# Scores computed twice, with the causal mask added inside VectorE's minimum, in a fused attention and mixture-of-experts kernel

## The chip, the cores and the metric

The program runs on one core of one Trainium2 chip. The metric is the device time of one execution in microseconds (us). Engines are named as in the profile: PE is TensorE's matmul queue and PEld its weight loads, DVE is VectorE, ACT is ScalarE, POOL is GpSimd, SP is the queue of SyncE, which here only issues DMAs.

## The reference

```python
B, S, D = 8, 512, 256          # 8 sequences of 512 tokens, 16 heads of 16
x = x + attention(x @ cond_weight[itok[b]].T + cond_bias[itok[b]])   # causal softmax(Q K^T / 4) V, then W_o
h = relu(x @ wi.T + two low-rank terms) @ wo.T + two low-rank terms   # 1024 hidden units
gates = softmax(h @ gate_w + gate_b); top 2 of 8 experts per token
out = x + sum over the two of gate * (gelu(gelu(h @ w1 + b1) @ w2 + b2) @ w3 + b3)
```

All of it is float32. For one head the attention is

```python
scores = Q @ K.T / DH ** 0.5 + triu(-inf, k=1)
out = softmax(scores, axis=-1) @ V
```

## The kernel before

The program has two parts. The first takes the 8 sequences one after the other. Round b does the attention of sequence b together with the feed-forward part of sequence b-1, so there are 9 rounds: round 0 has attention only, round 8 feed-forward only. The second part, which the change does not touch, sorts the tokens by expert and runs 71 tiles of 128 tokens through the experts.

A round has an **opening** and then a number of **steps**. In the opening PE makes q, k and v of the sequence (each product as three matmuls of a high and a low part), the products with `wo_sb` and `sel_sb`, and the first hidden units of the sequence before. Then come 35 steps. A step takes two units; a unit is one head of one tile of 128 queries, and there are 64. For each unit PE adds the mask to PSUM with a bf16 matmul (`mask_b`, `id_b`) and then the scores (`q_sb`, `k_sb`, 64 rows of the array, so that two heads stand above each other). DVE takes the negated maximum of the row (`nmax`), ACT computes the exponential and its sum (`probs`), PE transposes `probs` block by block (line 831), DVE or ACT copies the result to `probs_t`, and every other step PE multiplies four heads with `v_sb` into bank 6. Into each step goes one **filler**, a piece of the feed-forward work (`FILLERS`).

Every engine runs its own list in order; PSUM banks are handed over by two semaphores each (`filled` and `drained`, with `vacant` before a bank is used again). The score ring has banks 0, 1 and 2. The last product of a round before the next one opens is in bank 1 (`rt`).

Besides this the rounds split the experts' weights for the second part, 8 **pieces** of 128x512 a round, 64 in all. A piece goes through this circle, with one buffer `w_rest` and one buffer `w_high`: POOL issues the load of `w_rest` from HBM (line 1513); ACT rounds it to `w_high` (line 990, `cast`); POOL subtracts, in place (line 1516); POOL issues two stores to `wsplit` (line 1521); when both have landed, POOL issues the next load. ACT's `cast` stands at fixed places in ACT's list, two in the opening (`W_OPENING`) and six in the steps:

```python
W_OPENING = (0, 10)
W_STEPS = (2, 8, 14, 19, 23, 28)
...
            def cast(b, n):
                act.wait_ge(s_wpiece, b * (16 * W_PIECES) + 16 * (n + 1))
                nc.scalar.copy(w_high[:, :], w_rest[:, :]).then_inc(s_whigh, 1)
...
                if piece or not isinstance(b, int) or b:
                    pool.wait_ge(s_wsplit, n * 32)
```

## Time and profile before

| | |
|---|---|
| Median of 3 runs | 1509.88 us (1509.63 to 1516.31) |
| The profiled execution | 1507.66 us, of which the trace spans 1506.1 us |
| PE busy | 1359.4 us, 90% of the span |
| DVE, ACT, POOL busy | 875.0, 767.0, 420.0 us |
| Mean granted clock of PE | 0.955 of full speed |
| First part (rounds 0 to 8) | up to about 937 us |
| Exponentials on ACT, maxima on DVE | 266.0 us and 227.3 us |
| Transposes of `probs` on PE (x1280) | 203.1 us |

The span is what the trace covers; the profiled execution's own time is 1.6 us above it. Busy time of a group of instructions counts each moment once within the group, while neighbours overlap, so what an instruction costs in a full queue is the distance of the starts and not its duration.

### The profile page before, as it was taken

The numbers are of one execution on the slowest core, as the hardware profiler recorded it, in microseconds if no ns is written. First come the engines' busy times: TensorE is split into PE (matmuls) and PEld (weight loads), VectorE is DVE, ScalarE is ACT, GpSimd is POOL, SyncE is SP. The second block draws the span as 40 slices with busy tenths as digits, with TensorE's granted clock in tenths as the row PEclk, the third lists the DMA queues.
The fourth block names the chain that finished last, engine by engine and source line by source line (L and its number), as shares of the span: only waits on it lengthen the run. The fifth ranks groups of instructions, "written<-read, shape, count | busy, mean of one in ns | idle before, by whom it ended". The sixth has DMA issues, their size and how long they took to land.

```text
span 1506.1 us, 32247 instructions
## 1 busy us (share of the span) xinstructions
PE 1359.4 (90%) x10297; PEld 1053.1 (70%) x10298; DVE 875.0 (58%) x1945; ACT 767.0 (51%) x2003; POOL 420.0 (28%) x553
## 2 busy tenths in 40 slices
PE   5989999999989989999999988249899999999997
PEld 3556766766766766766766757238788888888886
DVE  3765665665665665665666662645455555555554
ACT  4776676665666665675666651013233333333332
POOL 2212211221221211211212210133344444444442
PEclk9799999999999999999999999559999999999999
DMA  6112222222222222222222220652624223342221
GB/s 221 64 66 97 76 82 98 78 96 82 78 95 83 77 81 93 77 86 98 78 80 77 79 72 29 271 225 36 247 42 145 42 42 88 101 148 40 38 40 13
DMA packets 50642, 137.85 MB, mean 92 GB/s; under 512 B 10514, under 2 KB 29586, under 8 KB 48882
## 3 DMA queue, kind: packets, MB, share of 16 engines
q0 software_dynamic: 28992, 68.35, 16.9%
q1 hardware_dynamic: 21554, 68.18, 12.3%
q8 instruction: 65, 1.06, 0.3%
q14 instruction: 31, 0.25, 0.1%
HBM read 86.03 MB, written 51.38 MB: 91 GB/s over the span
## 4 chain that ended last, share of the span: by engine, by line
PE 81%; DVE 5%; ACT 4%; issue 4%; DMA 4%; POOL 1%; SPq 0%; POOLq 0%; DVEq 0%; ACTq 0%
PE bank L665 66%; PE bank L831 9%; PE bank L924 4%; ACT probs L1092 3%; DVE nmax L1276 2%; PE bank L916 1%; DMA xg<-hrows,gid 1%; DMA w_rest<-in_w_all 1%; DMA wsplit<-w_rest 1%; POOL hit_v L1536 0%; PE bank L839 0%; ACT w_high L990 0%; DVE probs_t L1290 0%; POOL w_rest L1516 0%; PE bank L779 0%
## 5 line engine op out<-in xcount | busy, mean ns | idle before, releaser
L1092 ACT ACTIVATE probs<-bank,nmax 128x512 f32<-128x512 f32 (+3 forms) x512 | 266.0, 525 | 164.4 <-DVE nmax L1276 163.0
L1276 DVE TENSOR_REDUCE nmax<-bank 128x1 f32<-128x512 f32 (+3 forms) x512 | 227.3, 486 | 201.7 <-PE bank L665 201.3
L1128 ACT ACTIVATE g<-z 128x512 f32<-128x512 f32 x142 | 89.8, 632 | 281.3 <-DVE z L1466 270.0
L831 PE MATMUL bank<-id_f,probs 128*128 128x128 f32 x1280 | 203.1, 290 | 0.4 <-ACT probs_t L1100 0.4
L1516 POOL TENSOR_TENSOR w_rest<-w_rest,w_high 128x512 f32<-128x512 f32 x64 | 81.4, 1271 | 425.5 <-ACT w_high L990 425.5
L665 PE MATMUL bank<-wst,g1t_high 128*128 x568 | 186.0, 409 | 0.9 <-DVE g1t_low L1454 0.9
L831 PEld LDWEIGHTS bank<-id_f,probs 128*128 128x128 f32 x1280 | 137.8, 143 | 45.0 <-issue 24.2
L1558 POOL DMA_INDIRECT out<-y_sb,sid x71 | 114.3, 1610 | 149.7 <-PE bank L916 67.1
L1290 DVE COPY probs_t<-bank 128x128 f32<-128x128 f32 (+3 forms) x320 | 140.1, 454 | 12.6 <-PE bank L831 12.6
L1466 DVE TENSOR_TENSOR z<-bank,b_sb 128x512 f32<-128x512 f32 x142 | 98.2, 692 | 74.3 <-PE bank L665 63.2
L665 PEld LDWEIGHTS bank<-wst,g1t_high 128*128 128x128 f32 x568 | 102.5, 190 | 20.8 <-issue 1.1
L665 PE MATMUL bank<-wst,g1t_low 128*128 x284 | 113.4, 399 | 0.0
L665 PE MATMUL bank<-wst,g2t_high 128*128 x568 | 107.7, 289 | 1.5 <-DVE g2t_low L1454 1.5
L665 PE MATMUL bank<-k_sb,q_sb 64*128 64x512 f32 (+3 forms) x512 | 107.8, 418 | 0.0
L665 PE MATMUL bank<-mask_b,id_b 128*128 128x128 bf16 x512 | 84.6, 228 | 21.2 <-ACT probs L1092 17.4
L1092 ACT ACTIVATION_READ_ACCUMULATOR probs<-bank,nmax 128x1 f32 x512 | 101.3, 198 | 0.0
L665 PE MATMUL bank<-probs_t,v_sb 128*32 128x128 f32 x2560 | 98.4, 281 | 0.0
L665 PE MATMUL bank<-wst,xgt_high 128*128 x284 | 96.9, 423 | 1.3 <-DVE xgt_low L1454 1.3
L1513 POOL DMA_DIRECT2D w_rest<-in_w_all x64 | 35.0, 546 | 216.4 <-DMA wsplit<-w_rest 216.4
L1548 POOL DMA_INDIRECT xg<-hrows,gid x71 | 76.2, 1073 | 63.8 <-POOL gid L1545 56.8
L665 PEld LDWEIGHTS bank<-probs_t,v_sb 128*32 128x32 f32 x2560 | 62.9, 110 | 41.9 <-issue 28.4
L1100 ACT COPY probs_t<-bank 128x384 f32<-128x384 f32 (+3 forms) x192 | 88.3, 460 | 3.1 <-PE bank L831 2.9
(213 smaller groups left out, 2879.2 us busy)
## 6 DMA issues: line engine op xcount, KB each, us to landing
wst<-wsplit SPq DMA_DIRECT2D x8, 4096.0 KB, 12.6
w_rest<-in_w_all POOLq DMA_DIRECT2D x64, 256.0 KB, 3.1
wsplit<-w_high POOLq DMA_DIRECT2D x64, 256.0 KB, 2.3
wsplit<-w_rest POOLq DMA_DIRECT2D x64, 256.0 KB, 2.6
hrows<-h_sb SPq DMA_DIRECT2D x8, 528.0 KB, 3.0
x_in<-in_xT SPq DMA_DIRECT2D x8, 512.0 KB, 3.5
wb_raw<-in_lora_wb SPq DMA_DIRECT2D x8, 512.0 KB, 3.5
x_res<-in_xT SPq DMA_DIRECT2D x8, 512.0 KB, 4.5
```

The costliest lines, as they stand in the source:

```text
L665: return nc.tensor.matmul(*a, **k)
L831: ins = nc.tensor.transpose(at(n, rd)[:, kb * P:(kb + 1) * P], probs[:, t % 4, kb * P:(kb + 1) * P], id_f[:, :])
L924: ins = nc.tensor.transpose(bank[bt][:, k * P:(k + 1) * P], g[:, k * P:(k + 1) * P], id_f[:, :])
L1092: taken(nc.scalar.activation(probs[:, s % 4, 0:(i + 1) * P], at(n, rd)[:, 0:(i + 1) * P], ACT.Exp, bias=nmax[:, s % 8:s % 8 + 1], accum_ou ...
L1100: taken(nc.scalar.copy(probs_t[:, t % PT_SLOTS, 0:w], at(n, rd)[:, 0:w]), n, rd)
L1128: nc.scalar.activation(g[:, :], z[:, :], ACT.Gelu).then_inc(s_g, 1)
L1276: V.tensor_reduce(nmax[:, s % 8:s % 8 + 1], at(n, rd)[:, 0:(s // HEADS + 1) * P], AX.X, ALU.max, negate=True).then_inc(s_max, 1)
L1290: taken(V.tensor_copy(probs_t[:, t % PT_SLOTS, 0:w], at(n, rd)[:, 0:w]), n, rd)
L1466: V.tensor_tensor(z[:, :], bank[bl][:, :], bias[:, bass.ds(e, 1), :].rearrange("p o n -> p (o n)"), ALU.add).then_inc(s_z, 1)
L1516: nc.gpsimd.tensor_tensor(w_rest[:, :], w_rest[:, :], w_high[:, :].bitcast(F32), ALU.subtract).then_inc(s_wlow, 1)
L1548: nc.gpsimd.indirect_dma_start(xg[:, buffer, :], None, hrows, bass.IndirectOffsetOnAxis(ap=gid[:, 0:1], axis=0), bounds_check=B * S - 1, o ...
L1558: nc.gpsimd.indirect_dma_start(out_rows, bass.IndirectOffsetOnAxis(ap=sid[:, 0:1], axis=0), y_sb[:, buffer, :], None, bounds_check=B * S - ...
```

## The change

Two heads (a pair) are taken at a time over all 512 queries, in three chunks each, and the scores are computed twice. The first time they have the queries on the partitions: DVE adds a causal mask to the negated scores and keeps the minimum of each row, in one instruction per tile (`tensor_tensor_reduce`, which is followed by an instruction that reads the accumulator), so PE's mask matmul is gone. The minima go, as a high and a low part, through a matmul with an identity into two more rows of `q_sb` (rows 32, 33 and 96, 97), against ones in `k_sb`. The second time PE computes the scores with the keys on the partitions (`st`), with the maximum already in the sum: ACT takes the exponential straight into `probs_t`. So PE's transposes, the copies to `probs_t` and ACT's reads of its accumulator are gone. POOL zeroes what lies above the diagonal (`affine_select`, line 1578 of the new kernel, four of 128x256 for each pair). The row sums come out of the product with `v_sb`, which holds ones now; a matmul with `swap_sb` brings them beside the values (`nn`), and DVE takes the reciprocal of 128x512 and multiplies. A round has 34 steps; `FILL_COUNTS` says how many fillers each has. POOL's part is written out for all rounds, without a loop. The buffer `x_res` is gone, so `load_res` stands later in SP's list.

The casts: none in the opening, and one at steps 9, 12, 15, ..., 30.

```diff
-W_OPENING = (0, 10)
-W_STEPS = (2, 8, 14, 19, 23, 28)
...
+SCORE_CHUNKS = ((3,), (2, 0), (1,))
+KEY_CHUNKS = ((0,), (3, 1), (2,))
...
+M_LAG, ST_LAG, PV_LAG, NORM_LAG = 4, 5, 12, 20
+STEPS = NORM_LAG + 2 + 6 * (QUADS - 2)
...
+def work_at(step):
+
+
+    return (chunk_at(step), chunk_at(step - ST_LAG), every(step - M_LAG, CHUNKS, PAIRS),
+            every(step - PV_LAG, 2 * CHUNKS, QUADS), every(step - NORM_LAG, 4 * CHUNKS, KD))
...
+FILL_COUNTS = [2] * 5 + [1] * 7 + [0] + [1] * 5 + [0, 1, 0, 1, 1, 1, 0] + [2] * 5 + [0, 1, 0, 1]
...
+CAST_LAG = 9
```

PE, in each step:

```diff
+                    score, late, m, quad, norm = work_at(step)
+                    if score is not None:
+                        g, u = score
+                        if u == 0:
+                            drained(pe, ("qs", g), rd)
+                            drained(pe, ("ks", g), rd)
+                        for half in range(2):
+                            n = ("s", g, u, half)
+                            vacant(pe, n, rd)
+                        for c, (i, cols) in enumerate(query_tiles(u)):
+                            for half in range(2):
+                                n, r = ("s", g, u, half), STRIP * half
+                                ins = mm(at(n, rd)[:, cols], q_sb[r:r + STRIP, g, i * P:(i + 1) * P],
+                                         k_sb[r:r + STRIP, g, 0:(i + 1) * P], start=True, stop=True,
+                                         skip_group_check=True)
+                                if c == len(SCORE_CHUNKS[u]) - 1:
+                                    done(ins, n, rd)
+                    if late is not None:
+                        g, u = late
+                        if u == 0:
+                            drained(pe, ("m", g), rd)
+                        for half in range(2):
+                            vacant(pe, ("st", g, u, half), rd)
+                        for c, (kb, cols) in enumerate(key_tiles(u)):
+                            for half in range(2):
+                                n, r = ("st", g, u, half), STRIP * half
+                                ins = mm(at(n, rd)[:, cols], k_sb[r:r + STRIP, g, kb * P:(kb + 1) * P],
+                                         q_sb[r:r + STRIP, g, kb * P:S], start=True, stop=True, skip_group_check=True)
+                                if c == len(KEY_CHUNKS[u]) - 1:
+                                    done(ins, n, rd)
+                    if m is not None:
+                        n = ("m", m)
+                        vacant(pe, n, rd)
+                        pe.wait_ge(s_msplit, b * PAIRS + m + 1)
+                        for i in range(TB):
+                            ins = mm(at(n, rd)[:, i * P:(i + 1) * P], mm_sb[:, 2 * i:2 * i + P], id_r[:, :],
+                                     start=True, stop=True)
                         done(ins, n, rd)
...
+                    if norm is not None:
+                        n = ("nn", norm)
+                        vacant(pe, n, rd, [("pv", 2 * norm + 1)])
+                        done(mm(at(n, rd)[:, :], swap_sb[:, :], sums[:, :], start=True, stop=True), n, rd)
+                    for n_fill, piece in rd.fillers(step):
+                        product(rd, n_fill, piece)
+                    if quad is not None:
+                        n = ("pv", quad)
+                        vacant(pe, n, rd, [("v", t2) for t2 in range(TB // 2)] if quad == 0 else ())
+                        pe.wait_ge(s_pmask, 2 * (b * PAIRS + 2 * (quad + 1)))
+                        for kb in range(TB):
+                            for c in range(4):
+                                h = 4 * quad + c
+                                values = v_sb[:, kb, quad // 2, c, quad % 2:quad % 2 + 2, :]
+                                first = PT_AT[kb]
+                                ins = mm(at(n, rd)[PART * c:PART * (c + 1), kb * P:S],
+                                         values.rearrange("p a d -> p (a d)"),
+                                         probs_t[:, h % PT_SLOTS, first:first + S - kb * P],
+                                         start=(kb == 0), stop=(kb == TB - 1))
                         done(ins, n, rd)
```

ACT, in each step:

```diff
+                    _, late, m, quad, _ = work_at(step)
+                    if late is not None:
+                        g, u = late
+                        if u == 0 and g >= 3:
+                            filled(act, ("pv", (g - 3) // 2), rd)
+                        for half in range(2):
+                            n = ("st", g, u, half)
+                            width = key_tiles_width[u]
+                            filled(act, n, rd)
+                            taken(nc.scalar.activation(probs_t[:, (2 * g + half) % PT_SLOTS, S * u:S * u + width],
+                                                       at(n, rd)[:, 0:width], ACT.Exp, scale=-1.0), n, rd)
+                    if m is not None and m % 2 == 0:
+                        n = ("m", m)
+                        filled(act, n, rd)
+                        for half in range(2):
+                            rows = slice(STRIP * half + M_ROW, STRIP * half + M_ROW + 2)
+                            ins = nc.scalar.copy(q_sb[rows, m, :], at(n, rd)[rows, :])
+                        taken(ins, n, rd)
+                    for n_fill, piece in rd.fillers(step):
+                        take(rd, n_fill, piece)
+                    if quad is not None and quad % 2 == 0:
+                        n = ("pv", quad)
+                        if quad:
+                            filled(act, ("nn", quad // 2 - 1), rd)
+                        filled(act, n, rd)
+                        nc.scalar.activation(ot_sb[:, quad // 2, :], at(n, rd)[:, :], ACT.Identity, scale=marks_sb[:, 1:2])
+                        taken(nc.scalar.activation(sums[:, :], at(n, rd)[:, :], ACT.Identity, scale=marks_sb[:, 2:3]),
                               n, rd)
...
+                    cast_of = every(step - CAST_LAG, CHUNKS, PAIRS)
+                    if cast_of is not None:
+                        cast(b, cast_of)
                     if step in LORA_STEPS:
                         lora_high(b, *LORA_STEPS[step])
```

DVE, in each step:

```diff
+                    score, _, m, _, norm = work_at(step)
+                    quad = work_at(step - 1)[3]
+                    if quad is not None and quad % 2 == 1:
+                        n = ("pv", quad)
+                        drained(dve, ("pv", quad - 1), rd)
                         filled(dve, n, rd)
...
+                        V.scalar_tensor_tensor(ot_sb[:, quad // 2, :], at(n, rd)[:, :], marks_sb[:, 2:3],
+                                               ot_sb[:, quad // 2, :], ALU.mult, ALU.add)
+                        taken(V.scalar_tensor_tensor(sums[:, :], at(n, rd)[:, :], marks_sb[:, 1:2], sums[:, :],
+                                                     ALU.mult, ALU.add), n, rd)
+                    if score is not None:
+                        g, u = score
+                        for half in range(2):
+                            n = ("s", g, u, half)
+                            filled(dve, n, rd)
+                            dve.sem_inc(s_tick, 1)
+                            for i, cols in query_tiles(u):
+                                ins = V.tensor_tensor_reduce(at(n, rd)[:, cols], at(n, rd)[:, cols],
+                                                             mask_w[:, S - (i + 1) * P:S], 1.0, 2.0 * BIG,
+                                                             ALU.add, ALU.min, nmax[:, g % 2, half, i:i + 1])
+                            taken(ins, n, rd)
+                        if u == CHUNKS - 1:
+                            drained(dve, ("s", g, u, 1), rd)
+                            if g > 0:
+                                filled(dve, ("m", g - 1), rd)
+                            V.tensor_scalar(m_parts(0), nmax[:, g % 2, :, :], -1.0, None, ALU.mult).then_inc(s_mhigh, 1)
+                            dve.wait_ge(s_mhigh, b * PAIRS + g + 1)
+                            V.scalar_tensor_tensor(m_parts(1), nmax[:, g % 2, :, :], -1.0, m_parts(0).bitcast(F32), ALU.mult,
+                                                   ALU.subtract).then_inc(s_msplit, 1)
+                    if m is not None and m % 2 == 1:
+                        n = ("m", m)
+                        filled(dve, n, rd)
+                        for half in range(2):
+                            rows = slice(STRIP * half + M_ROW, STRIP * half + M_ROW + 2)
+                            ins = V.tensor_copy(q_sb[rows, m, :], at(n, rd)[rows, :])
+                        taken(ins, n, rd)
                     if norm is not None:
...
+                        n = ("nn", norm)
                         filled(dve, n, rd)
...
+                        taken(V.reciprocal(rt_sb[:, :], at(n, rd)[:, :]), n, rd)
+                        drained(dve, n, rd)
+                        V.tensor_tensor(ot_sb[:, norm, :], ot_sb[:, norm, :], rt_sb[:, :], ALU.mult).then_inc(s_ot, 1)
+                    for n_fill, piece in rd.fillers(step - 1) if step > 0 else ():
                         take(rd, n_fill, piece)
                     if step in LOW_STEPS:
```

POOL:

```diff
+            def allowed(rd, g, u, tiles):
...
+                drained(pool, ("st", g, u, 1), rd)
+                at_0, at_1 = (PT_AT[kb] // P for kb in tiles)
+                for half in range(2):
+                    blocks = probs_t[:, (2 * g + half) % PT_SLOTS, :].rearrange("p (n c) -> p n c", c=P)
+                    diag = blocks[:, at_0:at_1 + 1:at_1 - at_0, :]
+                    ins = nc.gpsimd.affine_select(diag, diag, [[0, 2], [1, P]], ALU.is_ge, 0.0, base=0,
+                                                  channel_multiplier=-1)
+                ins.then_inc(s_pmask, 1)
...
+            def load_piece(b, piece):
+                cols = slice(piece * W_PIECE, (piece + 1) * W_PIECE)
+                if b or piece:
+                    pool.wait_ge(s_wsplit, (b * W_PIECES + piece) * 32)
+                pool.dma_start(w_rest[:, :], w_all[b:b + 1, :, cols].rearrange("o p n -> (o p) n")).then_inc(s_wpiece, 16)
...
+            def split_piece(b, piece):
                 n = b * W_PIECES + piece
                 cols = slice(piece * W_PIECE, (piece + 1) * W_PIECE)
...
                 pool.wait_ge(s_whigh, n + 1)
                 nc.gpsimd.tensor_tensor(w_rest[:, :], w_rest[:, :], w_high[:, :].bitcast(F32), ALU.subtract
                                         ).then_inc(s_wlow, 1)
                 pool.wait_ge(s_wlow, n + 1)
...
                 for part, src in enumerate((w_high[:, :].bitcast(F32), w_rest[:, :])):
...
+                    pool.dma_start(wsplit[b:b + 1, :, part, cols].rearrange("o p n -> (o p) n"), src
                                    ).then_inc(s_wsplit, 16)
 
...
+            for b in range(B):
+                rd = Round(b)
+                for g in range(PAIRS):
+                    allowed(rd, g, 1, (0, 3))
+                    load_piece(b, g)
+                    allowed(rd, g, 2, (1, 2))
```

What the change makes of ACT's list between two casts. Rows of before, a round with feed-forward work, two casts that follow each other in the steps:

```order
L990 CAST w_high<-w_rest 128x512
L1092 ACTIVATE probs,rsum<-bank,nmax 128x256 x2
L1092 ACTIVATE probs,rsum<-bank,nmax 128x384 x2
L1100 COPY probs_t<-bank 128x256
L1092 ACTIVATE probs,rsum<-bank,nmax 128x384 x2
L1100 COPY probs_t<-bank 128x384
L1115 COPY rt_sb<-bank 128x256
L1092 ACTIVATE probs,rsum<-bank,nmax 128x384 x2
L1100 COPY probs_t<-bank 128x384
L1092 ACTIVATE probs,rsum<-bank,nmax 128x384 x2
L1100 COPY probs_t<-bank 128x384
L990 CAST w_high<-w_rest 128x512
```

Rows of the change, the same engine and a round of the same kind, from one cast to the one after the next (`q_sb` here is the copy of the minima, 2x512):

```order
L1019 CAST w_high<-w_rest 128x512
L1128 ACTIVATE probs_t<-bank 128x256 x2
L1128 ACTIVATE probs_t<-bank 128x512 x4
L1019 CAST w_high<-w_rest 128x512
L1128 ACTIVATE probs_t<-bank 128x256 x2
L1135 CAST q_sb<-bank 2x512 x2
L1128 ACTIVATE probs_t<-bank 128x512 x4
L1019 CAST w_high<-w_rest 128x512
```

Between these two casts ACT had the work of five steps; now it has six exponentials, the work of three steps.

POOL's list for one piece, before:

```order
L1513 DMA w_rest<-in_w_all 128x512
L1516 TENSOR_TENSOR w_rest<-w_rest,w_high 128x512
L1521 DMA wsplit<-w_high 128x512
L1521 DMA wsplit<-w_rest 128x512
L1513 DMA w_rest<-in_w_all 128x512
```

and after:

```order
L1586 DMA w_rest<-in_w_all 128x512
L1578 AFFINE_SELECT probs_t<-probs_t 128x2x128 x2
L1592 TENSOR_TENSOR w_rest<-w_rest,w_high 128x512
L1596 DMA wsplit<-w_high 128x512
L1596 DMA wsplit<-w_rest 128x512
L1578 AFFINE_SELECT probs_t<-probs_t 128x2x128 x2
L1586 DMA w_rest<-in_w_all 128x512
```

The circle of a piece stands as it was; two selects have come in on each side of the load.

PE's list at the end of a round, after the change (`gw_sb` is the gate, `sums` the `nn` product in bank 0, `wq_high` the next round's first product, also in bank 0):

```order
L684 MATMUL bank<-probs_t,v_sb 32x512 x4
L684 MATMUL bank<-probs_t,v_sb 32x384 x4
L684 MATMUL bank<-probs_t,v_sb 32x256 x4
L684 MATMUL bank<-probs_t,v_sb 32x128 x4
L684 MATMUL bank<-gw_sb,ht_sb 128x8 x8
L684 MATMUL bank<-sums,swap_sb 128x512
L684 MATMUL bank<-cond_high,wq_high 128x512
```

Between the `nn` product and the next opening PE has nothing any more, and the opening's first product takes the bank of `nn`.

## Rows read from the trace of the kernel before

**Rows 1.** Timeline of PE, first instructions of rounds and of round 0's steps (start, duration).

```profile
32.63 0.27 PE L665 MATMUL bank<-mask_b,id_b 128*128 128x128 bf16 x2 [1.74 <-DVE k_sb L1198]
...
111.77 0.47 PE L665 MATMUL bank<-cond_high,wq_high 128*128 128x512 f32 x1 [1.48 <-DVE cond_low L1188]
...
785.51 0.47 PE L665 MATMUL bank<-cond_high,wq_high 128*128 128x512 f32 x1 [1.56 <-issue]
...
890.55 5.33 PE L665 MATMUL bank<-ot_sb,wo_sb 128*128 128x512 f32 x8 [1.46 <-DVE ot_sb L1282]
```

**Rows 2.** Windows, round 3's opening and steps: us, PE, PEld, DVE, ACT, POOL, PEclk.

```profile
331.90:359.00 27.10, 24.41 (x122) 17.21 (x122) 14.44 (x25) 12.55 (x25) 5.81 (x8) 0.94 0.37 127
359.00:442.00 83.00, 79.63 (x769) 58.94 (x768) 53.61 (x132) 56.50 (x174) 17.50 (x24) 1.00 0.22 75
```

**Rows 3.** Chain that ended last, round 3, one piece (start, duration).

```profile
403.76 1.29 POOL w_rest L1516
406.35 4.38 DMA wsplit<-w_rest
410.94 0.53 issue
411.49 3.09 DMA w_rest<-in_w_all
```

**Rows 4.** Timeline of POOL, round 0, the shortest circle of a piece.

```profile
28.58 1.28 POOL L1516 TENSOR_TENSOR w_rest<-w_rest,w_high 128x512 f32<-128x512 f32 x1 [3.54 <-ACT w_high L990]
...
31.01 0.54 POOL L1521 DMA_DIRECT2D wsplit<-w_rest  x1
34.19 0.54 POOL L1513 DMA_DIRECT2D w_rest<-in_w_all  x1 [2.64 <-DMA wsplit<-w_rest]
38.22 1.27 POOL L1516 TENSOR_TENSOR w_rest<-w_rest,w_high 128x512 f32<-128x512 f32 x1 [3.49 <-ACT w_high L990]
```

**Rows 5.** Waits, whole span (us in total, times, longest).

```profile
POOL w_rest L1513 <- DMA wsplit<-w_rest: 216.4, 63, 6.1
...
ACT w_high L990 <- DMA w_rest<-in_w_all: 13.5, 9, 2.2
```

**Rows 6.** Timeline of ACT, the second cast of round 3's opening.

```profile
345.78 0.62 ACT L990 CAST w_high<-w_rest 128x512 fp32r<-128x512 f32 x1 [1.38 <-DMA w_rest<-in_w_all]
```

**Rows 7.** Windows, PE's gap in that opening and behind it.

```profile
344.00:348.00 4.00, 1.39 (x11) 0.62 (x10) 1.69 (x4) 2.48 (x5) 1.26 (x1) 0.97 0.17 55
348.00:352.00 4.00, 4.00 (x16) 3.32 (x16) 1.24 (x3) 0.60 (x1) 1.10 (x2) 0.61 0.36 131
```

**Rows 8.** Timeline of PE, a step with 512-wide tiles and the gate.

```profile
322.16 0.51 PE L665 MATMUL bank<-k_sb,q_sb 64*128 64x512 f32 x2
322.60 1.09 PE L831 MATMUL bank<-id_f,probs 128*128 128x128 f32 x8
323.53 1.02 PE L665 MATMUL bank<-x_in,wc_sb 128*128 128x512 f32 x2
324.48 1.08 PE L665 MATMUL bank<-probs_t,v_sb 128*32 128x128 f32 x32
...
326.42 1.85 PE L665 MATMUL bank<-gw_sb,ht_sb 128*128 128x8 f32 x16
```

**Rows 9.** Timeline of PE, two matmuls of 512 columns back to back.

```profile
353.46 0.39 PE L665 MATMUL bank<-x_low,wi_high 128*128 128x512 f32 x1
353.69 0.39 PE L665 MATMUL bank<-x_high,wi_low 128*128 128x512 f32 x1
```

**Rows 10.** Groups by line and form, round 3, ACT and DVE (busy, mean ns).

```profile
L1092 ACT ACTIVATE probs<-bank,nmax 128x512 f32<-128x512 f32 x16 | 10.9, 685 | 5.5 <-DVE nmax L1276 5.5
...
L1276 DVE TENSOR_REDUCE nmax<-bank 128x1 f32<-128x512 f32 x16 | 10.3, 686 | 7.0 <-PE bank L665 7.0
...
L1301 DVE RECIPROCAL rinv<-rsum 128x16 f32<-128x16 f32 x4 | 1.0, 246 | 0.0
...
L1241 DVE RECIPROCAL ginv<-gsum 128x4 f32<-128x4 f32 x1 | 0.2, 178 | 0.0
```

356 lines of the change are left out of this document (137 added, 219 removed).

## The prediction

> **What bounds the kernel now.** I read the rounds first. PE's first instruction of round 1 is at 111.77 us, that of round 7 at 785.51, and round 8 begins its product with `wo_sb` at 890.55 [rows 1]: rounds 1 to 6 take (785.51 - 111.77) / 6 = 112.3 us each, round 0's steps 79.1 us (from 32.63), round 7 up to that product 105.0 us. The windows over round 3 show PE busy for 24.4 of 27.1 us in the opening and 79.6 of 83.0 us in the steps, at a granted clock of 0.94 and 1.00, with DVE and ACT at about 54 and 57 of those 83 us [rows 2]. So PE sets the pace. But the chain through the same round leaves PE once, for a piece of the expert weights: POOL's subtraction at 403.76, the landing of its stores, the next load, 3.09 us until that has landed [rows 3]. This second limit lies close below the first, and the change moves both.
>
> **The circle of a piece.** From the subtraction of one piece to that of the next nothing can overlap, since `w_rest` is one buffer. The shortest in the trace runs from 28.58 to 38.22, 9.64 us [rows 4]: 2.97 us from the subtraction to the end of the second store's issue apart from the wait, 2.64 us until the stores have landed, 4.03 us from the load's issue to the next subtraction, with ACT's cast in it. The wait for the stores is 216.4 / 63 = 3.43 us on the mean [rows 5]; in round 3 the part from the load on is 3.8 us (3.09 us of landing [rows 3], the cast of 0.62 us [rows 6] and a handover of 0.1). I take 2.97 + 3.43 + 3.9 = **10.3 us**. Eight of them fit into 112.3 us, so ACT waited for a load only 9 times in 64, 13.5 us in all [rows 5].
>
> **What three steps cost now.** After the change eight casts stand at steps 9, 12, ..., 30: seven circles must pass within 21 steps. What would the 21 steps take without them? PE loses, per round, 160 transposes at 0.93 / 8 = 0.116 us, 18.6 us; 32 mask pairs at about 0.2 us (0.27 us busy [rows 1]), 6.7 us; and the `rt` transposes, 1 us. It gains the second scores, 24 pairs of chunks at no more than 0.44 us, 10.6 us; 32 identity products, priced as transposes of the same size, 3.7 us; and two `nn` products at 0.95 us, 1.9 us [rows 8]. The columns through `v_sb` are as many as before. That is 10 us less, 94 us of PE in a round of which 22 us are opening: 34 steps at 2.1 us, three steps about **6.4 us**. The circle needs 10.3. ACT waits at each cast, and behind the cast in its list stand the exponentials of the next steps; their PSUM banks (4 and 5, one chunk's worth) stay full, and PE can go about one step further. So the circle sets the pace of steps 9 to 30.
>
> DVE stays under this. Per pair of heads it has eight fused instructions over 2560 columns, at the reduction's 686 ns for 512 [rows 10] about 3.9 us with the accumulator reads, and some 1.5 us of small work. That this instruction is as fast as the reduction is not shown anywhere; were it to take twice as long, a pair would cost some 9 us, still below 10.3. POOL's four selects per pair are one-input operations on 256 columns; the nearest row is its subtraction of 512 with two inputs, 1.27 us [rows 4], so between half of that and all, 0.64 to 1.27 us. Two stand in the wait for the stores (3.43 us) and two in the wait for load and cast (3.3 us); up to 1.3 us each, both waits cover them. I take 0.64.
>
> **A round after the change, from PE's first product.**
> - Opening: 27.1 us now. The cast in it kept ACT for 1.38 + 0.62 = 2.0 us [rows 6], in front of `low_i`; PE stood still for 2.6 of the 4 us from 344 and ran the next 4 us at a clock of 0.61 [rows 7], which loses 4 x 0.39 = 1.6 us. With the cast gone, 2.0 and 1.6 us go: 23.5 us.
> - Steps 0 to 8: nine score chunks and four second ones at 0.44, two identity groups 0.9 us, 44 matmuls of 512 columns at 0.23 us [rows 9] and 16 transposes: 18.7 us, and a tenth at each change of work, 20 us; a wait of about 1 us for the copy of the minima, which DVE makes behind its minima. Step 9 up to the cast: scores 0.9 us and two exponentials of at most 0.69 us [rows 10], 2.2 us. Together 23.2 us.
> - Seven circles: 72.1 us.
> - End: the product with `v_sb` of the last four heads waits for POOL's selects of the last pair, which stand behind the last load: 0.7 + 2.97 + 3.43 + 0.54 + 1.3 = 8.9 us after the cast before the last, 1.4 us ahead of the last cast. It has 40 blocks of 128 columns where the row has 16 in 1.0 us [rows 8], 2.6 us; gate 1.8 us; `nn` 0.95 us. Then PE has nothing to do: the next round's first product takes the bank of `nn`, which DVE frees only when the reciprocal is done. Its price is not in the trace for this size: 16 elements take 246 ns and 4 take 178 ns [rows 10], 5.7 ns an element, so 178 + 508 x 5.7 = 3.1 us; were it an ordinary operation, 0.69 us. The two rows point to the long one and I take it. End: 7.2 us after the last cast.
> - The gap before the opening is as long as the one in rows 7, so 1.6 us more at the lower clock.
>
> Sum: 23.5 + 1.6 + 23.2 + 72.1 + 7.2 = 127.6 us, 15.3 us more than 112.3. Six rounds: +92 us. Round 0: about 22.5 us to the first cast (DVE's fused instructions and the base weights' low parts set it), 72.1 and 5.4 us without a gate, 100.0 against 79.1: +21 us. Round 7: 128.4 up to the product with `wo_sb` against 105.0: +23 us. A microsecond for the longer preparation of round 0. In all +137 us on the span of 1506.1 us, that is 1643; outside of it lie 1.6 us (1507.66), and the median of the runs shown is 2.2 us above that execution: **1647 us**.
>
 The two small rows give 5.4 cycles an element; no row has the large size.
>
> **Rivals.**
> 1. PE goes on setting the pace and the kernel is faster. For it speaks that PE is the bound in rows 2 and loses 10 us a round. Then a round takes some 13 us less (10, the 3.6 us of the opening, less 1 for the reciprocal), and the kernel 1507.7 - 8 x 13 = 1404 us. It needs a circle that ends within three steps; what decides is 112.3 = 55.5 + 7 x circle, 8.1 us. Against it: the shortest of 63 is 9.64 us, and nothing in it has been removed. 0.04. A circle of about 8.1 us, no change: 0.03.
> 2. The steps are even slower than the circle. PE works 6.4 us in each 10.3 us and stands still twice in two circles, since every second one it also waits for the selects before the product with `v_sb` (8.9 us after a cast). Behind that wait stand this product, two steps and the next chunk, 8.9 us at full clock: 17.8 of 20.6 us. At half clock they are 16.8 us and two circles 25.7 us, 18 us more a round, 1790 us at worst. Rows 7 show the clock back after 4 us of dense work, so I give it 0.12, for 1715 to 1790 us. The Trainium skill (TensorE: Matmul & The Clock Gate, section on HAM oscillation) describes just such a kernel, in which a DMA wait between short bursts leaves every burst at the lower clock; the trace so far shows single gaps alone.
> 3. All is as I say, but every circle takes the shortest time and the rest of the round shrinks more: 1520 to 1590 us, 0.05.
>
> **How the numbers follow.** The forecast has 0.76, with a range of its own of 1590 to 1715 us. Below: all 56 circles at 9.64 us, -37 us, and the reciprocal at 0.69 us, -19 us. Above: every wait for the stores as in rows 3, from 406.35 + 0.54 to 411.49, 4.6 us and so 1.2 us more than the mean, +67 us. To hold 8 in 10 it takes in a little of rival 2: 1590 to 1725. A measurement of this kernel tells about 0.5%, 8 us. Faster 0.04, same 0.03, slower 0.93.
>
> **What the profile after will show.** If I am right: ACT's cast waits for the load of `w_rest` some 56 times, 3 to 5 us each, and this pair leads the list of waits; casts 10.3 us apart within a round; the chain made of landings of `wsplit` and `w_rest` for the greater part of the first 1050 us; PE busy well under 0.8 there, with a clock between 0.7 and 0.95; DVE's reciprocal near 3 us with PE idle behind it. Wrong would be: casts 6 to 7 us apart (the DMAs land sooner when they are issued from written-out code), or casts more than 12 us apart with ACT waiting for PE or for POOL instead. The second part must take the same 570 us as now.

## The result and the profile after

| | before | after |
|---|---|---|
| median of the runs | 1512.78 us | 1694.95 us |
| range of the runs | 1509.63 to 1516.31 (4) | 1686.55 to 1696.32 (4) |
| ratio | | 1.1206, interval 1.115 to 1.1261 |
| span of the profiled execution | 1506.1 us | 1684.8 us |
| rounds 1 to 6, each | 112.3 us [rows 1] | 133.7 us |
| round 7 up to the product with `wo_sb` | 105.0 us [rows 1] | 131.1 us |

The kernel is 12% slower; the forecast was 1647 us (1590 to 1725) and slower.

The page of the changed kernel, lines of its parts 1, 2 and 4 (busy time; PE's granted clock in 40 slices; the chain by engine and by line):

```profile
PE 1350.7 (80%) x7705; PEld 991.3 (59%) x7706; DVE 919.2 (55%) x2297; ACT 646.5 (38%) x1236; POOL 517.4 (31%) x809
...
PEclk8578877977978987978978897775899999999998
...
PE 60%; DMA 12%; DVE 11%; POOL 6%; issue 6%; ACT 4%; SPq 0%; POOLq 0%; DVEq 0%; ACTq 0%
```

The digits of the clock have a pattern that repeats with the rounds: two or three slices of 8 or 9 and then 7. The windows over rounds 1 to 6 say it in one number. The first fence is the kernel before, the second the changed one (us, then PE, PEld, DVE, ACT, POOL, PEclk, share of the DMA engines, GB/s):

```profile
111.77:785.51 673.74, 631.69 (x5521) 460.51 (x5521) 420.37 (x958) 430.87 (x1224) 139.93 (x192) 0.99 0.25 85
```

```profile
137.93:940.14 802.21, 628.72 (x3576) 415.42 (x3577) 452.17 (x1218) 338.95 (x645) 214.15 (x384) 0.84 0.20 70
```

PE has 35% fewer matmul records and the same busy time, because each takes longer. The share of the clock that was not granted is (1 - 0.84) x 802 = 128 us of these six rounds, against 7 us before. That is more than what it costs, since PE also stands still for 173 us of them (42 before), and a low clock costs nothing while it does. The same work on PE at a clock of 0.99 takes 547 us (run 11 below, 3579 records), so the lower clock makes PE's own work 629 - 547 = 82 us longer, 14 us a round.

The waits of the changed kernel (us in total, times, longest), which answer to [rows 5]:

```profile
ACT w_high L1019 <- DMA w_rest<-in_w_all: 115.3, 31, 8.0
...
POOL w_rest L1586 <- DMA wsplit<-w_rest: 96.5, 56, 5.1
PE bank L684 <- POOL probs_t L1578: 96.3, 23, 12.4
...
PE bank L684 <- DVE nmax L1335: 56.8, 51, 4.3
...
PE bank L684 <- DVE rt_sb L1357: 24.8, 7, 3.5
...
PE bank L684 <- DVE q_sb L1352: 22.7, 24, 1.0
```

ACT waited 9 times for a load before, now 31 times. PE's own waits are new kinds: for POOL's selects (in front of the product with `v_sb`), for DVE's minima, for the reciprocal and for DVE's copy of the minima into `q_sb`.

The eight casts of round 3 in ACT's timeline of the changed kernel (the second cast of a round in [rows 6] is the one that answers):

```profile
458.34 0.62 ACT L1019 CAST w_high<-w_rest 128x512 fp32r<-128x512 f32 x1
...
470.38 0.62 ACT L1019 CAST w_high<-w_rest 128x512 fp32r<-128x512 f32 x1
...
479.00 0.62 ACT L1019 CAST w_high<-w_rest 128x512 fp32r<-128x512 f32 x1 [1.12 <-DMA w_rest<-in_w_all]
...
487.66 0.62 ACT L1019 CAST w_high<-w_rest 128x512 fp32r<-128x512 f32 x1 [2.78 <-DMA w_rest<-in_w_all]
...
499.54 0.62 ACT L1019 CAST w_high<-w_rest 128x512 fp32r<-128x512 f32 x1
...
514.00 0.62 ACT L1019 CAST w_high<-w_rest 128x512 fp32r<-128x512 f32 x1
...
524.30 0.62 ACT L1019 CAST w_high<-w_rest 128x512 fp32r<-128x512 f32 x1 [3.56 <-DMA w_rest<-in_w_all]
...
532.95 0.62 ACT L1019 CAST w_high<-w_rest 128x512 fp32r<-128x512 f32 x1 [6.12 <-DMA w_rest<-in_w_all]
```

Four gaps end in a wait for the load, the second, third, sixth and last, and three, of 11.9 to 14.5 us, do not. Three of the four are 8.6 and 8.7 us long; the sixth is 10.3 us. Over the eight rounds the seven gaps add up to 73.9 us on the mean; by place they are 11.4, 8.6, 8.8, 10.6, 14.3, 11.0 and 9.0 us. The second gap in the chain that ended last, and the load of the sixth:

```profile
471.08 1.29 POOL w_rest L1592
472.37 0.29 issue
472.65 0.56 POOL wsplit L1596
473.21 2.58 DMA wsplit<-w_rest
475.79 0.29 issue
476.08 2.90 DMA w_rest<-in_w_all
478.97 0.02 issue
479.00 0.63 ACT w_high L1019
...
519.82 4.46 DMA w_rest<-in_w_all
```

It is the circle of [rows 3], shorter than there by 2.58 us of landing where 4.38 us stood, and 0.29 us to the next load where it was 0.53. The landing in [rows 3] is a late one: the pages of both kernels have the same median for this store (KB each, median us from issue to landing).

```profile
wsplit<-w_rest POOLq DMA_DIRECT2D x64, 256.0 KB, 2.6
```

The sixth gap is a circle too, one in which the load took 4.46 us to land instead of 2.90. And the end of the round in PE's timeline:

```profile
531.48 3.96 PE L684 MATMUL bank<-probs_t,v_sb 128*32 128x512 f32 x32 [7.48 <-POOL probs_t L1578]
535.38 1.95 PE L684 MATMUL bank<-gw_sb,ht_sb 128*128 128x8 f32 x16
537.18 1.10 PE L684 MATMUL bank<-sums,swap_sb 128*128 128x512 f32 x2
541.83 0.77 PE L684 MATMUL bank<-cond_high,wq_high 128*128 128x512 f32 x1 [3.54 <-DVE rt_sb L1357]
542.39 0.63 PE L684 MATMUL bank<-cond_low,wq_high 128*128 128x512 f32 x1
542.82 0.63 PE L684 MATMUL bank<-cond_high,wq_low 128*128 128x512 f32 x1
```

PE waits 7.48 us for the last selects, then 3.54 us for the reciprocal, and the products behind it follow each other at 0.43 us instead of the 0.23 us of [rows 9]: half clock.

### The profile page after: what moved, and what is told of

Its sections match the earlier page's. It is cut to its first block, busy times and chain, and to the rows that moved or that the text cites. A ratio compares the mean times of both kernels' runs of the same rounds, so it can differ in the third digit from the quotient of the medians.

```text
span 1684.8 us, 26627 instructions
## 1 busy us (share of the span) xinstructions
PE 1350.7 (80%) x7705; PEld 991.3 (59%) x7706; DVE 919.2 (55%) x2297; ACT 646.5 (38%) x1236; POOL 517.4 (31%) x809
## 4 chain that ended last, share of the span: by engine, by line
PE 60%; DMA 12%; DVE 11%; POOL 6%; issue 6%; ACT 4%; SPq 0%; POOLq 0%; DVEq 0%; ACTq 0%
PE bank L684 55%; DMA wsplit<-w_rest 6%; PE bank L953 4%; DMA w_rest<-in_w_all 3%; DVE rt_sb L1357 3%; POOL w_rest L1592 3%; DVE bank L1335 3%; ACT w_high L1019 1%; POOL wsplit L1596 1%; DVE q_sb L1352 1%; POOL probs_t L1578 1%; PE bank L945 1%; DMA xg<-hrows,gid 1%; ACT probs_t L1128 1%; POOL w_rest L1586 1%
## 5 line engine op out<-in xcount | busy, mean ns | idle before, releaser
L1335 DVE CUSTOM_DVE_ANT_0 bank<-bank,mask_w 128x512 f32<-128x512 f32 (+3 forms) x512 | 240.6, 517 | 134.5 <-PE bank L684 133.2
L1128 ACT ACTIVATE probs_t<-bank 128x512 f32<-128x512 f32 (+1 forms) x384 | 181.1, 524 | 223.0 <-PE bank L684 222.0
L1578 POOL TENSOR_SCALAR_AFFINE_SELECT probs_t<-probs_t 128x256 f32<-128x256 f32 x256 | 98.5, 414 | 389.2 <-ACT probs_t L1128 387.9
L684 PE MATMUL bank<-probs_t,v_sb 128*32 128x512 f32 (+3 forms) x1024 | 109.2, 584 | 97.4 <-POOL probs_t L1578 96.3
L1592 POOL TENSOR_TENSOR w_rest<-w_rest,w_high 128x512 f32<-128x512 f32 x64 | 81.4, 1272 | 270.4 <-ACT w_high L1019 270.4
L684 PE MATMUL bank<-q_sb,k_sb 64*128 64x512 f32 (+3 forms) x512 | 104.1, 444 | 42.1 <-DVE q_sb L1352 22.7
L684 PEld LDWEIGHTS bank<-k_sb,q_sb 64*128 64x128 f32 x512 | 53.0, 220 | 113.9 <-issue 85.0
L684 PEld LDWEIGHTS bank<-q_sb,k_sb 64*128 64x128 f32 x512 | 59.5, 236 | 69.4 <-DVE q_sb L1352 32.0
L684 PE MATMUL bank<-wf_high,hid_high 128*128 128x256 f32 x256 | 91.8, 359 | 0.0
L684 PEld LDWEIGHTS bank<-wst,g2t_high 128*128 128x128 f32 x568 | 86.7, 190 | 1.8 <-issue 1.7
L953 PE MATMUL bank<-id_f,g 128*128 128x128 f32 x568 | 85.8, 274 | 2.4 <-ACT g L1167 2.4
```

The costliest lines, as they stand in the source:

```text
L684: return nc.tensor.matmul(*a, **k)
L953: ins = nc.tensor.transpose(bank[bt][:, k * P:(k + 1) * P], g[:, k * P:(k + 1) * P], id_f[:, :])
L1128: taken(nc.scalar.activation(probs_t[:, (2 * g + half) % PT_SLOTS, S * u:S * u + width], at(n, rd)[:, 0:width], ACT.Exp, scale=-1.0), n, rd)
L1335: ins = V.tensor_tensor_reduce(at(n, rd)[:, cols], at(n, rd)[:, cols], mask_w[:, S - (i + 1) * P:S], 1.0, 2.0 * BIG, ALU.add, ALU.min, nma ...
L1578: ins = nc.gpsimd.affine_select(diag, diag, [[0, 2], [1, P]], ALU.is_ge, 0.0, base=0, channel_multiplier=-1)
L1592: nc.gpsimd.tensor_tensor(w_rest[:, :], w_rest[:, :], w_high[:, :].bitcast(F32), ALU.subtract).then_inc(s_wlow, 1)
```

## The experiments

Each row is read against the kernel before on the same chip, so the last column can be compared between them.

| run | median, us | ratio (interval) | above before, us |
|---|---|---|---|
| changed kernel | 1694.95 | 1.1206 (1.115 to 1.1261) | +182 |
| 1 before, casts at the new steps | 1623.14 | 1.0746 (1.0708 to 1.0785) | +115 |
| 2 changed, no splitting | 1547.12 | 1.0259 (1.0233 to 1.0285) | +39 |
| 3 changed, two buffers | 1639.89 | 1.0872 (1.0834 to 1.0909) | +131 |
| 4 changed, `nn` in bank 6 | 1673.44 | 1.1083 (1.1054 to 1.1112) | +165 |
| 5 changed, mask by PE | 1721.51 | 1.1372 (1.1336 to 1.1407) | +208 |
| 6 before, no splitting | 1487.47 | 0.9833 (0.9801 to 0.9865) | -26 |
| 7 changed, two buffers, late load | 1574.30 | 1.0387 (1.0349 to 1.0426) | +61 |
| 8 changed, selects first | 1635.34 | 1.0809 (1.0761 to 1.0857) | +122 |
| 9 changed, no reciprocal | 1645.52 | 1.0884 (1.0837 to 1.093) | +134 |
| 10 changed, casts spread | 1563.13 | 1.0337 (1.0301 to 1.0373) | +52 |
| 11 run 10 and three edits | 1460.22 | 0.9658 (0.963 to 0.9685) | -51 |
| 12 run 11, reciprocal whole | 1483.09 | 0.9812 (0.9784 to 0.984) | -27 |

**The theory** is that of the forecast: the places of the casts make the circle of a piece the pace. **The rivals:** the new computation has waits of its own that would hold the pace without any piece; or PE's lower clock does.

**Run 1, the places alone.**

```diff
-W_OPENING = (0, 10)
-W_STEPS = (2, 8, 14, 19, 23, 28)
+W_OPENING = ()
+W_STEPS = (9, 12, 15, 18, 21, 24, 27, 30)
```

> The kernel before with nothing changed but the steps of its eight casts: none in the opening, and steps 9, 12, ..., 30 as in the changed kernel. If the circle of a weight piece sets the pace of the steps by where the casts stand, seven circles of 9.6 to 10.3 us take the place of 21 steps at 2.4 us: a round gains 17 to 22 us in the steps and loses 3.6 us in the opening, so 13 to 18 us a round and 1610 to 1660 us in all, casts about 10 us apart with ACT waiting for the load at nearly all 56 of them. If it is the new way of computing the scores, and not the places, that costs the time (long chains between the engines, with PE at half clock behind them), the places cost nothing here: 1513 us, 8 us to either side.

The kernel before loses 115 us by these two lines. Its seven gaps between casts are 72.2 us a round on the mean, 10.3 us each, where the forecast had 72.1. ACT's casts waited for a load:

```profile
ACT w_high L990 <- DMA w_rest<-in_w_all: 131.4, 51, 6.5
```

So the mechanism is shown, by itself and with its size, in the kernel before. What part it has in the changed kernel is for the other runs to show.

**Runs 2 and 6, both kernels without the splitting.** In the changed kernel the cast goes and POOL's load, subtraction and stores become copies from DRAM to DRAM; the kernel before likewise, at its own places.

```diff
-                    cast_of = every(step - CAST_LAG, CHUNKS, PAIRS)
-                    if cast_of is not None:
-                        cast(b, cast_of)
...
-                    load_piece(b, g)
+                    cols = slice(g * W_PIECE, (g + 1) * W_PIECE)
+                    for part in range(2):
+                        pool.dma_start(wsplit[b:b + 1, :, part, cols], w_all[b:b + 1, :, cols]).then_inc(s_wsplit, 16)
                     allowed(rd, g, 2, (1, 2))
-                    split_piece(b, g)
```

> The changed kernel without the splitting of the expert weights: no cast on ACT, no load, subtraction or wait on POOL; POOL copies each piece twice from DRAM to DRAM instead, so the second part computes with unsplit weights and wrong low parts. If the circle sets the pace, the steps fall to the pace of PE (6.4 us for three steps) or a little more, 7 to 8 us: 15 to 20 us less a round and a shorter wait at its end, 1450 to 1540 us in all. If the chains of the new computation hold the pace by themselves (minimum, split, product, copy, second scores; exponentials, selects, product with v_sb), it stays above 1640 us. If PE's lower clock holds it, the waits for weights go but the mean clock of the steps stays below 0.85, and it takes 1560 to 1640 us.

> The kernel before without the splitting of the expert weights, as in the run of the changed kernel without it: no casts, loads, subtractions; DRAM to DRAM copies at the old places of the casts; the second part computes with unsplit weights. If PE set the pace before, only the 3.6 us of each opening and some ACT waits come back: 1475 to 1500 us, so that the changed kernel without the splitting (1547 us) is the slower one by 50 to 70 us, a loss that has nothing to do with the pieces. If the pieces cost the kernel before as much as the changed one (about 148 us), it would be near 1365 us.

The pieces cost the changed kernel 182.2 - 38.6 = 143.6 us and the kernel before 25.6 us. So 118 of the 182 us are the pieces, the circle and what hangs on it, and 38.6 + 25.6 = 64 us are the new computation without any piece. That second part I had not forecast: with the pieces gone I expected 1450 to 1540 us. The windows over its rounds 1 to 6:

```profile
122.61:809.98 687.37, 598.18 (x3576) 400.18 (x3577) 444.06 (x1218) 314.02 (x597) 122.23 (x288) 0.89 0.21 64
```

A round takes 114.6 us and the clock is 0.89; PE's own work takes 598 - 547 = 51 us longer than at a clock of 0.99, in these six rounds. The rivals are not right as they stood, but both hold a part.

The exponentials in ACT's timeline show where the 19.1 us lie that a round of the changed kernel takes more than a round of run 2 (means of rounds 1 to 6). From the last exponential of step 9 to that of step 27 it is 58.6 us against 50.8, in the one step from there to step 28 it is 7.9 against 2.3, and from the last exponential to the next round's first product 17.9 against 11.7; up to step 9 there is nothing between them. So without any piece three steps take 50.8 / 6 = 8.5 us and not 6.4, as long as one circle of the changed kernel, and more than half of what the pieces cost falls behind step 27.

**Runs 3, 7 and 8, where the pieces' 144 us go.** Run 3 and 7 have two buffers for `w_rest`. To make room the high part isn't kept: the stored weights are not the split ones, all instructions and bytes are. Run 8 moves only the load in POOL's list:

```diff
-                    load_piece(b, g)
                     allowed(rd, g, 2, (1, 2))
+                    load_piece(b, g)
                     split_piece(b, g)
```

> The changed kernel with two buffers for w_rest, so that the load of the next piece is issued while this one is being worked on; to make room, the high part is not kept apart: ACT copies in place, POOL subtracts the buffer from itself and both stores read the same buffer (the same instructions and bytes, other values in the split weights). Every piece of work of the circle is still there, only the landings are off its path. If it is the landings in the circle, 1470 to 1570 us and within 30 us of the run without the splitting. If it is POOL's or ACT's work on the pieces that holds the steps up, it is within 40 us of the changed kernel, 1655 to 1700 us.

> The run with two buffers for w_rest (same values left out), but each load is issued behind both selects of its pair, and not between them; in the first version POOL still waited 105.9 us for the landing of stores that it had just issued, in front of the second select. Now both landings are off every list. If landings were what was left, 1550 to 1590 us, near the run without the splitting. If POOL's subtraction and its issues hold PE up through the selects, 1625 to 1650 us, as with the first version.

> The changed kernel with one buffer and all its values, and only POOL's order changed: both selects of a pair, then the wait for the stores and the load, then the subtraction. PE waits for selects 96.3 us in all. If it is the wait for the stores in front of the select that makes the product with v_sb late, this gives 40 to 90 us (1605 to 1655 us). If the circle is the pace, the load now also waits for the second select, the circle becomes longer and the kernel is no faster: 1690 to 1750 us, with ACT waiting for loads more than the 115.3 us of now.

Run 3 gave 51 us and met neither expectation: the load was off the path, but POOL still waited 105.9 us for stores that it had just issued, and the second select stood behind that wait. With the load behind both selects (run 7) another 70 us came, as expected of landings, and 23 us are left above the run without splitting for the work itself (cast, subtraction, issues). Run 8 has one buffer and all values and gains 60 us by order alone. PE's waits for the selects in run 8 and in run 7:

```profile
PE bank L684 <- POOL probs_t L1578: 48.1, 8, 8.6
```

```profile
PE bank L683 <- POOL probs_t L1578: 19.7, 8, 5.7
```

In the changed kernel they were 96.3 us in 23 places, 70.6 us of them at the eight ends of a round (7.48 us in the fence above). In run 8 only those eight are left, one in each round, and they are shorter. Its circle did not become longer by waiting for the second select: the seven gaps are 70.2 us against 73.9, and the first and the fourth fall from 11.4 and 10.6 us to 9.4 and 9.5.

**Runs 4 and 9, the reciprocal.**

```diff
-            take(("nn", norm), "score")
+            take(("nn", norm), "pv")
```

> The changed kernel with the two products of the sums with swap_sb in bank 6, that of the product with v_sb, which is drained by then, and not in the ring of the scores; so the next round's first product no longer waits for the reciprocal. If the reciprocal at the end of a round stands on the path as in the trace (24.8 us over 7 rounds, with PE at half clock for some 9 us behind it), this gives 25 to 45 us: 1650 to 1670 us. If the time at the end of a round is set by the weight pieces or by the wait for ot_sb further on, which takes the reciprocal's place, it gives less than 8 us.

Run 9 has `V.tensor_copy` in the place of `V.reciprocal`.

> The changed kernel with the two reciprocals of a round (512 columns, 3358 ns each in the trace) replaced by a copy; the heads are then not normalised. A copy of this size takes 690 ns, so DVE's list is 2.7 us shorter at two places of each round. At the end of a round PE waits 3.5 us for it: that gives about 19 us over 7 rounds. In the middle PE waited 2.75 to 3.15 us for minima behind it, between the fifth and the sixth cast, where the gap of the casts was 14.5 us: if that gap is the reciprocal's and not a landing's, another 20 us and some half clock, 1635 to 1655 us in all; if a landing or a select takes its place there, 1665 to 1680 us.

Bank 6 gave 17 us against the kernel before of its chip (21.5 between the medians), between my two expectations: PE's wait of 24.8 us went, but six waits for `ot_sb`, 9.5 us in all, took its place in part, and little of the clock came back (0.86 over rounds 1 to 6). Without the reciprocals the kernel is 48 us faster, so the one in the middle of a round costs at least as much as the one at its end. The gaps of the casts say the same: the fifth falls from 14.3 to 11.7 us, 21 us over eight rounds. Ahead of the result I had counted only the reciprocal at the end.

**Run 5, the mask back on PE.** Eight matmuls of the identity with the mask for a pair, and a plain minimum:

```diff
-                                ins = V.tensor_tensor_reduce(at(n, rd)[:, cols], at(n, rd)[:, cols],
-                                                             mask_w[:, S - (i + 1) * P:S], 1.0, 2.0 * BIG,
-                                                             ALU.add, ALU.min, nmax[:, g % 2, half, i:i + 1])
+                                ins = V.tensor_reduce(nmax[:, g % 2, half, i:i + 1], at(n, rd)[:, cols], AX.X, ALU.min)
```

> The second part of the change undone: in the changed kernel TensorE adds the mask to the diagonal block of each tile (a product of the identity with the mask behind the scores, 8 a pair of heads), and VectorE takes the minimum with a plain reduction. By the trace the instruction that adds and takes the minimum costs 714, 582, 442 and 330 ns and each has an accumulator read of 138 ns behind it, so DVE should be relieved of about 1.3 us per pair, 10 us a round, and PE gets 0.5 to 1 us more per pair. If the pieces' circle and POOL hold the pace, nothing comes of it: 1680 to 1705 us. If DVE's minima do (PE waits for them 56.8 us in all), 1640 to 1670 us.

Slower by 26 us, which neither expectation had. The groups by form in a round, of the changed kernel and then of this run:

```profile
L1335 DVE CUSTOM_DVE_ANT_0 bank<-bank,mask_w 128x512 f32<-128x512 f32 x16 | 10.8, 714 | 6.9 <-PE bank L684 6.9
...
L1335 DVE DVE_READ_ACCUMULATOR2_ANT nmax<- 128x1 f32 x64 | 8.8, 138 | 0.1
```

```profile
L1342 DVE TENSOR_REDUCE nmax<-bank 128x1 f32<-128x512 f32 x16 | 10.3, 683 | 6.9 <-PE bank L685 6.9
...
L685 PE MATMUL bank<-mask_w,id_b 128*128 128x128 bf16 x64 | 9.6, 234 | 0.0
```

The fused instruction is nearly as fast as the reduction (714 and 683 ns); the accumulator read of 138 ns is most of what it costs more, 8.8 us a round. By all groups of the two kinds DVE's part falls from 40.9 to 29.6 us a round, as expected, and PE gets 9.6 us of busy time; the kernel becomes 3.3 us a round slower. Over rounds 1 to 6 PE is busy for 51 us more and stands still for 23 us less. My reading, not shown by a run of its own, is that PE's work between two waits is on the path even here, and that DVE's mostly is not. In this kernel, at least, this half of the change is a gain, of 26 us.

**Runs 10 to 12, toward a kernel that beats both.** Run 10 keeps every value and spreads the casts: one in the opening, seven in steps five apart, with POOL's list sorted by the same steps.

```diff
+W_OPENING = 10
+W_STEPS = (1, 6, 11, 16, 21, 26, 31)
+LOAD_LAG = 1.9
...
+                for piece, step in enumerate(W_STEPS, 1):
+                    todo += [(step + 0.5, "split", piece), (step + 0.5 + LOAD_LAG, "load", piece + 1)]
+                for _, what, m in sorted(todo, key=lambda t: t[0]):
```

> The changed kernel, all its values kept, with the eight casts of a round spread out: one in the opening (behind its eleventh piece of work) and seven at steps 1, 6, 11, ..., 31, and POOL's list in the order of these steps: the subtraction and the stores behind the cast, the wait for their landing and the next load some two steps later, behind the selects due before it. A circle then has five steps, about 12 us. If the places of the casts in the lists are what cost the time, both landings are now hidden: 1545 to 1580 us, near the two runs without landings (1547 and 1574 us). If it costs as much wherever it stands, 1635 us or more.

It gains 130 of the 144 us that the pieces cost, as expected; PE's waits for selects fall to a single one of 1.2 us. PE's timeline in the second half of a round, the rows with a wait of 0.8 us and more:

```profile
432.56 0.38 PE L686 MATMUL bank<-k_sb,q_sb 64*128 64x256 f32 x2 [0.81 <-DVE nmax L1338]
...
440.57 0.39 PE L686 MATMUL bank<-k_sb,q_sb 64*128 64x256 f32 x2 [1.30 <-DVE nmax L1338]
441.90 0.50 PE L686 MATMUL bank<-q_sb,k_sb 64*128 64x512 f32 x2 [0.95 <-DVE q_sb L1355]
...
449.30 0.80 PE L686 MATMUL bank<-k_sb,q_sb 64*128 64x384 f32 x4 [2.96 <-DVE nmax L1338]
...
478.74 0.77 PE L686 MATMUL bank<-cond_high,wq_high 128*128 128x512 f32 x1 [3.54 <-DVE rt_sb L1360]
```

and the windows around the third of these rows and behind it:

```profile
436.00:440.00 4.00, 3.27 (x44) 2.21 (x32) 3.03 (x10) 0.78 (x3) 2.12 (x5) 1.00 0.41 135
440.00:442.00 2.00, 0.48 (x4) 0.31 (x4) 1.92 (x7) 0.00 (x0) 0.00 (x0) 1.00 0.20 72
442.00:446.00 4.00, 4.00 (x16) 2.63 (x16) 3.61 (x7) 2.30 (x5) 0.06 (x1) 0.66 0.00 0
446.00:450.00 4.00, 1.03 (x8) 0.77 (x7) 3.76 (x6) 0.38 (x1) 3.03 (x5) 0.50 0.17 63
450.00:454.00 4.00, 4.00 (x19) 3.11 (x18) 2.09 (x11) 1.94 (x5) 1.29 (x3) 0.50 0.36 122
454.00:458.00 4.00, 4.00 (x27) 2.34 (x30) 1.19 (x6) 2.05 (x4) 0.40 (x2) 0.63 0.03 11
```

The clock falls to 0.50 (1.2 GHz) ahead of the wait of 2.96 us: behind the short waits of 1.30 and 0.95 us, which stand close together. So run 11 takes on the short waits too: `nn` in bank 6, the first reciprocal in three parts in three steps, and the copies of the minima all on ACT, since on DVE they stand behind the minima of the next chunk.

> The run before with three more edits, all values kept: the products of the sums in bank 6, the first reciprocal of a round cut into 192, 160 and 160 columns in three successive steps, and both kinds of copies of the minima on ACT and none on DVE. Bank 6 gave 21.5 us by itself; PE's wait of 3 us behind the first reciprocal and half of the waits for DVE's copy (24.2 us in all) should give 10 to 30 us more: 1500 to 1545 us. Below 1505 us it would beat the kernel before; if it stays above 1540 us, PE's lower clock behind the waits that are left is the price of the new computation.

1460 us: 3.4% faster than the kernel before, and 40 us below the lower end of what I expected. The three edits are worth 103 us. The windows of rounds 1 to 6 in runs 10, 11 and 12 (one fence each):

```profile
129.38:831.65 702.27, 602.77 (x3576) 404.72 (x3577) 454.47 (x1218) 337.84 (x645) 213.43 (x384) 0.88 0.24 80
```

```profile
118.75:735.65 616.90, 547.18 (x3579) 361.80 (x3577) 415.23 (x1181) 362.29 (x695) 212.67 (x384) 0.99 0.27 92
```

```profile
122.82:757.27 634.45, 555.07 (x3579) 372.08 (x3577) 418.57 (x1169) 362.56 (x694) 212.41 (x384) 0.97 0.27 89
```

The clock is back at 0.99. Of the 85 us by which these six rounds become shorter from run 10 to run 11, 603 - 547 = 56 us are PE's own work, nearly the same number of matmuls (3576 and 3579) at the higher clock, and 30 us are time in which PE stood still. Run 12 takes one edit back, the reciprocal in three parts:

> The best run (1460 us) with one edit undone: the first reciprocal of a round is again one instruction over 512 columns. In the spread run PE waited 3.0 us for the minima behind it, once a round, and then ran at a clock of 0.50 to 0.56 for some 14 us. If only the wait itself counts, 8 rounds lose 3 us each and this gives 1484 us, 8 us to either side. If the lower clock behind the wait is the larger part of its price, each round loses another 4 to 7 us: 1515 to 1540 us, with a mean clock below 0.92 against 0.936.

```profile
513.56 0.39 PE L686 MATMUL bank<-k_sb,q_sb 64*128 64x256 f32 x2 [1.30 <-DVE nmax L1338]
...
520.54 0.79 PE L686 MATMUL bank<-k_sb,q_sb 64*128 64x384 f32 x4 [3.60 <-DVE nmax L1338]
```

It costs 23 us, 2.9 us a round, and 1483 us is what I expected if only the wait itself counts. The windows above do not quite bear that out: of the 17.6 us that rounds 1 to 6 take more than in run 11, 9.7 us are time in which PE stood still, and 7.9 us are the same matmuls at the lower clock. PE's waits for minima are 63.0 us in all against 46.0, but part of them takes the place of other waits. So the number was met by two smaller parts and not by 3 us of waiting a round. My second theory, that the clock behind the long wait is the larger part of its price and brings 1515 us or more, falls, but the clock is close to half of it. The long wait is longer than in run 10 (3.60 us), but the 0.95 us ahead of it is gone, and the clock stays at 1.00 until 518 us, where the long wait has begun. By windows of 2 us it is then at 0.50 until about 526 us, 7 us, where in run 10 it was so for 13 us. The two runs differ in bank 6 as well, so the missing short wait is the likely cause of this and not a shown one. The other 80 us of the 103 come from bank 6 and the copies on ACT together; how they share them was not measured.

## Why the prediction was right, and where its numbers were off

**The mechanism** is the one forecast, in part. Run 1 shows it alone in the kernel before. In the changed kernel the seven gaps of a round take 73.9 us against 72.1, but this agreement is luck, as the next two points show.

**The circle, 10.3 us.** In the kernel before it is right to the tenth on the mean (run 1). In the changed kernel it takes 8.6 us, below even the 9.64 us of rival 3. The next load is issued 2.3 us after the end of the stores' issue (491.02 to 493.34 in POOL's timeline) where the mean wait was 3.43 us. This mean had late landings in it; the median landing is the same in both kernels, 2.6 us. POOL's handovers are shorter as well: 0.30 us from the subtraction to the first store where it was 0.73 in rounds 1 to 7, and 0.29 us to the load where it was 0.53. The loop on POOL is the smaller part of this. Round 0 is written out in the kernel before too, its handover is 0.60 us, and it is there that the 9.64 us of [rows 4] were measured. The kernel before has an instruction more between each of these two waits and the issue behind it, `pool.sem_inc(s_tick, 1)`, which the changed kernel leaves out; no run took it away alone. With 8.6 us for each circle and nothing else changed, the forecast would have been 7 x 1.7 x 8 = 95 us lower, 1552 us and outside of its own range. The sum of the seven came out only because the first, fourth and fifth gap, between 10.6 and 14.3 us, are not the circle's, and late landings make the sixth 11.0 us.

**"ACT waits at each cast, some 56 times."** It waited 31 times, at four casts of a round. At the other casts ACT was late itself. The step that failed is the assumption that the steps' own pace, 6.4 us for three, lies well below the circle everywhere. That counts PE's work alone: with the waits for minima and copies, the mid-round reciprocal and the lower clock, three steps take 8.5 us even with no piece (run 2), and the circle 8.6. That the circle sets the pace of steps 9 to 30 as a whole is therefore only half true. It sets four of the seven gaps, is in the first and the fourth through POOL's late selects (run 8: 60 us in all by order alone), and the fifth, 14.3 us, has the reciprocal in it (run 9: 11.7 us).

**The lower clock.** I took 1.6 us at one place of a round. It makes PE's own work 82 / 6 = 14 us a round longer; part of that falls where PE would have waited. My rival 2 had it as the cause of 1715 to 1790 us with a chance of 0.12; the kernel came out at 1695, between my sum and the lower end of that rival. The Trainium skill (TensorE: Matmul & The Clock Gate, section on HAM oscillation) describes this for DMA waits between short bursts. The trace agrees behind the waits for the selects, which stand behind a landing (7.48 us, and half clock after it), and run 10 shows it as well with no such wait, behind short waits for DVE. I had weighed it against single gaps ([rows 7]), which was the wrong row to judge a chain of gaps by.

**The parts of the round outside the circles,** 55.5 us in the forecast, are 59.6 us on the mean. In round 3: from the first product to the first score 25.6 us, forecast 25.1 with its half clock; from there to the first cast 24.8 us instead of 23.2; the end 8.9 us instead of 7.2, of which 1.4 us is the product with `v_sb` (3.96 us instead of 2.6, at half clock behind its wait).

**The reciprocal,** 3.1 us: it took 3.358 us with PE idle behind it for 3.54 us, seven times. The Trainium skill (VectorE: DVE Perf Modes, section on the 8-slice pipeline) led to an estimate of 4.3 us; the measurement decides for 3.36, or 6.6 ns an element. What I missed is that the first one of a round stands in DVE's list ahead of the minima of the next chunk, for which PE waits.

**The fused instruction,** priced like the reduction: 714 against 683 ns for 512 columns, right. But a pair of heads takes 40.9 / 8 = 5.1 us where I had 3.9 us with the accumulator reads, which are 1.1 us of it. **The selects,** 0.64 us each: 0.41 us. **The second part** of the program: 614 us from the product with `wo_sb` to the end, 616 before, unchanged as forecast. **Round 0:** +26 us on 22 forecast, **round 7** +26 us on 23.

**Rival 1** (PE sets the pace, 1404 us) is excluded by run 2 even for a kernel without pieces: 1547 us. But run 11 shows it to be a target: 102.8 us a round, where the forecast had 99 for it.

## What to carry to other kernels

A change that takes work from the engine that sets the pace is worth nothing before the next limit has been moved too. Here eight circles of transfers had 112 us for 82 us of work, and the new places of eight small casts left seven of them 21 steps, which the forecast had at 45 us; in an in-order list, a wait for a transfer belongs behind everything that is due before it. Count short waits as well as long ones: behind two waits of 1.30 and 0.95 us close together the clock stayed down for 13 us (run 10), while with one of 3.60 us that had no such wait right ahead of it it was down for 7 us, from inside the wait on (run 12). And when a forecast adds up, look at its terms all the same: here a circle was taken 1.7 us too long and the steps beside it 2.1 us too short, and the sum came out.
